# Reordering one pair's work in the pipelined recurrence: what TensorE, ScalarE, VectorE and GpSimd do two pairs ahead

## The reference

```python
xa = layernorm(x); sx = previous_row(xa) - xa
xxx = tanh((xa + sx * maa_x) @ maa_w1)             # low rank, 5 x 32
xm = xa + sx * (maa_stack + xxx @ maa_w2)           # five mixtures: k, w, v, r, g
w = exp(-exp(time_decay + tanh(xw @ td_w1) @ td_w2))
r, k, v, g = xr @ Wr.T, xk @ Wk.T, xv @ Wv.T, silu(xg @ Wg.T)
s = s * w_t + k_t v_t ; out_t = r_t . (u * k_t v_t + s_before)   # scan over 128 tokens, 32 heads of 8 x 8
x1 = x + (groupnorm(out) * g) @ Wo.T
xc = layernorm(x1); sx2 = previous_row(xc) - xc
rr = sigmoid((xc + sx2 * maa_r) @ Wfr.T); kk = relu((xc + sx2 * maa_k) @ Wfk.T) ** 2
return x1 + rr * (kk @ Wfv.T)                       # the feed-forward part
```

## Time and profile before

| | us |
|---|---|
| median of 3 runs (2198.15 to 2201.47) | 2199.23 |
| the profiled execution's own time | 2204.45 |
| its span, first to last instruction | 2202.7 |
| mean granted TensorE clock over the span | 0.955 of full |
| recurrence stage within the span | about 1837 to 2202.7 |

### The profile page before, as it was taken

The page is one execution under the profiler, slowest core; times in us unless marked ns, Lnnn a source line. Parts: engine busy times, 40 slices in busy tenths (PEclk is TensorE's granted clock), DMA queues, the critical chain, the costliest instruction groups (busy, mean ns, idle before and its releaser), DMA issues. The chain is left out here.

```text
span 2202.7 us, 41115 instructions
## 1 busy us (share of the span) xinstructions
PE 1982.4 (90%) x15672; PEld 1724.6 (78%) x15672; DVE 1282.7 (58%) x2577; ACT 1085.0 (49%) x2926; POOL 529.4 (24%) x359
## 2 busy tenths in 40 slices
PE   5997898798999999999899999999979896888975
PEld 4675676796999999999699999999969884565653
DVE  5886787235555555555565554555533374888883
ACT  3775687563534433443454333433356432466653
POOL 3543554454200000000240000000025323324230
PEclk9998999899999999999999999999989997899986
DMA  4001000400000000002200000000120000000000
GB/s 164 2 2 30 21 11 2 153 1 6 6 6 5 0 5 5 5 5 87 72 6 6 0 5 5 5 5 0 46 69 1 11 29 0 1 6 10 6 10 10
DMA packets 33884, 44.90 MB, mean 20 GB/s; under 512 B 2178, under 2 KB 25828, under 8 KB 33508
## 3 DMA queue, kind: packets, MB, share of 16 engines
q1 hardware_dynamic: 33764, 43.26, 5.8%
HBM read 32.76 MB, written 2.10 MB: 16 GB/s over the span
## 5 line engine op out<-in xcount | busy, mean ns | idle before, releaser
L815 DVE TENSOR_TENSOR w_head_lo<-banks,w_head_hi 128x512 fp32r<-128x512 f32 x128 | 88.2, 691 | 249.3 <-ACT w_head_hi L727 241.7
L781 DVE TENSOR_TENSOR arena<-banks,cols 128x512 f32<-128x512 f32 x128 | 88.5, 692 | 227.3 <-PE banks L118 227.2
L746 ACT ACTIVATE arena<-banks 128x512 f32<-128x512 f32 x128 | 74.7, 595 | 296.4 <-PE banks L605 292.1
L524 POOL TENSOR_TENSOR w_hT_lo<-arena,w_hT_hi 128x512 fp32r<-128x512 f32 x16 | 20.9, 1304 | 821.6 <-ACT w_hT_hi L701 821.6
L739 ACT ACTIVATE arena<-banks,arena 128x129 f32<-128x129 f32 x512 | 180.6, 374 | 39.8 <-DVE arena L795 39.8
L989 POOL TENSOR_TENSOR arena<-arena 128x1024 f32<-128x1024 f32 x64 | 150.3, 2375 | 139.1 <-DVE arena L1248 139.1
L727 ACT ACTIVATE w_head_hi<-banks 128x512 fp32r<-128x512 f32 x128 | 76.4, 597 | 196.6 <-PE banks L615 196.5
L1182 ACT ACTIVATE arena<-arena 128x128 f32<-128x128 f32 x512 | 162.5, 394 | 3.5 <-DVE arena L1257 3.4
L116 PE MATMUL banks<-w_wo_lo,w_head_hi 128*128 128x256 f32 x512 | 148.6, 290 | 1.3 <-DVE w_head_lo L815 1.3
L116 PE MATMUL banks<-w_hT_lo,w_hi 128*128 128x256 f32 x512 | 146.6, 286 | 0.0
L116 PE MATMUL banks<-w_kv_lo,w_hi 128*128 128x256 f32 x512 | 145.2, 284 | 0.2
(11 more groups left out here) (300 smaller groups left out, 5831.0 us busy)
## 6 DMA issues: line engine op xcount, KB each, us to landing
arena<-ctx_t SPq DMA_DIRECT2D x32, 256.0 KB, 2.5
arena<-in_L_xattn_wq SPq DMA_DIRECT2D x8, 512.0 KB, 4.8
arena<-in_L_xattn_wk SPq DMA_DIRECT2D x8, 512.0 KB, 5.9
arena<-in_L_xattn_wv SPq DMA_DIRECT2D x8, 512.0 KB, 7.4
arena<-in_L_xattn_wo SPq DMA_DIRECT2D x8, 512.0 KB, 9.7
x<-in_x SPq DMA_DIRECT2D x4, 512.0 KB, 5.4
arena<-in_L_xattn_w SPq DMA_DIRECT2D x2, 1024.0 KB, 11.2
ctx_t<-in_ctx_t SPq DMA_DIRECT2D x1, 2048.0 KB, 12.5
```

Source lines behind the costliest of these rows:

```text
L746: act.activation(probT[:, b, :, :], bank[5 + b][:, :].rearrange("p (h q) -> p h q", h=HG), ACT.Copy).then_inc(probT_ok, 1)
L781: dve.tensor_tensor(qT[:, h:h + 2, :], bank[use % 2][:, :].rearrange("p (h t) -> p h t", h=2), core.col(bias, g * HG + h, 2)[:, :, None].t ...
L815: dve.tensor_tensor(head_lo[:, two, :], bank[5 + half][:, :].rearrange("p (h t) -> p h t", h=2), head_hi[:, two, :], ALU.subtract).then_in ...
```

## The change

Only the order of the steps within a slot changes, with one wait more on GpSimd; no instruction of arithmetic is added or taken away.

- TensorE: a_transpose(p + 2) moves from behind project_rr to ahead of project_kk; a_low(p + 2) moves from between centre and variance to right behind project_ff, ahead of unit 3's sum_heads, spread_v(p + 1, 0) and bonus_sums.
- ScalarE: tanh_low comes ahead of square_centred; normalise(p + 2) moves up ahead of row_rstd; copy_xa(p + 2) moves ahead of square_relu and sigmoid_rr.
- VectorE: shift_a(p + 2) moves ahead of unit 3.
- GpSimd: multiply_rk(a) also waits until kv_ok has reached 4a, which is when weigh_keys of unit 3 of the pair before has ended.

```diff
--- before.py
+++ after.py
@@ -1878,6 +1878,7 @@
                 gp.wait_ge(read["r"], a + 1)
                 gp.wait_ge(read["k"], a + 1)
                 wait(gp, ready["c"], a)
+                wait(gp, kv_ok, a * UNITS)
                 gp.tensor_tensor(rk[:, :, :], rT[:, parity(a), :, :], kT[:, parity(a), :, :], ALU.mult).then_inc(rk_ok, 1)
 
             def add_xa(a, fs):
@@ -2110,13 +2111,14 @@
                     c_transpose(p - 1)
                 if u:
                     sum_heads(p, 2)
+                if exists(p + 2):
+                    a_transpose(p + 2)
                 if c:
                     project_kk(p - 1)
                     project_rr(p - 1)
+                    project_ff(p - 1)
                 if exists(p + 2):
-                    a_transpose(p + 2)
-                if c:
-                    project_ff(p - 1)
+                    a_low(p + 2)
                 if u:
                     sum_heads(p, 3)
                 if a:
@@ -2126,9 +2128,6 @@
                     bonus_sums(p + 1)
                 if u:
                     centre(p)
-                if exists(p + 2):
-                    a_low(p + 2)
-                if u:
                     variance(p)
 
             core.wait_loaded(pe, stage, "maa_w1", "maa_w2", "maa_w2g")
@@ -2259,11 +2258,10 @@
 
             def slot(p):
                 u, a, c = exists(p), exists(p + 1), exists(p - 1)
-                if c:
-                    square_centred(p - 1)
                 if a:
                     tanh_low(p + 1)
                 if c:
+                    square_centred(p - 1)
                     group_rstd(p - 1)
                 if u:
                     make_decay(p, 2)
@@ -2276,6 +2274,8 @@
                     copy_v(p + 1)
                 if u:
                     make_decay(p, 3)
+                if exists(p + 2):
+                    normalise(p + 2)
                 if c:
                     row_rstd(p - 1)
                 if a:
@@ -2290,12 +2290,10 @@
                 if a:
                     make_decay(p + 1, 0)
                 if exists(p + 2):
-                    normalise(p + 2)
+                    copy_xa(p + 2)
                 if c:
                     square_relu(p - 1)
                     sigmoid_rr(p - 1)
-                if exists(p + 2):
-                    copy_xa(p + 2)
                 if u:
                     copy_raw(p)
                 if a:
@@ -2442,10 +2440,10 @@
                     make_gate(p + 1)
                 if c:
                     shift_c(p - 1)
+                if exists(p + 2):
+                    shift_a(p + 2)
                 if u:
                     unit(p, 3)
-                if exists(p + 2):
-                    shift_a(p + 2)
                 if c:
                     gate_ff(p - 1)
```

## The result

| | before | changed |
|---|---|---|
| median of 7 runs, us | 2200.72 | 2206.28 |
| lowest to highest, us | 2198.15 to 2201.47 | 2204.08 to 2210.02 |
| the profiled execution's own time, us | 2204.45 | 2204.08 |
| its span, us | 2202.7 | 2202.4 |

The ratio is 1.0028, with a 95% interval of 1.0016 to 1.0040: 6 us slower, 3.5 to 8.8. The forecast was 2203.5 in a range of 2194 to 2210.

A forecast was written before the change was run, and what follows sets the result against it. Neither TensorE nor VectorE alone was taken as the bound, but a loop passing between them. Slots -2.8, start +3.9 and clock +3.2 gave +4.3 on 2199.2, so 2203.5 us, range 2194 to 2210.

The forecast's parts named there:

- The new loop, 37.04 us at full clock: Slots 1 to 5: the loop from one VectorE mix to the next takes 37.04 us, against 37.6 before.
- Slot -1, +2.5 with 4.4 as the upper bound: Slot -1: spread_v behind a_low starts VectorE's unit 0 1.4 us later, plus 1.1 for clock; +4.4 if all at half clock.
- the 1.1 us for the clock: Slot -1: 1.1 us added for half clock after TensorE's idling, since a 2.07 us gap was followed by half clock.
- Slot 0, +1.4: Slot 0: unit 3's heads come 3.9 us later; the mix is +2.65 at the same clock, +0.1 at full; +1.4 taken.
- The slots, -2.8: Slots 1 to 5: a loop of 37.04 us against 37.6, five times, saves 2.8 us.
- two such drops more than before: Slots 1 to 5: two more clock drops around the mixing products, at 1.6 us each: +3.2, bounds 0 and +8.
- rival 4: It does nothing: project_kk stays at half clock, unit 3's heads 0.8 us later, slots 37.8, total 2201.7 us; chance 0.10.
- Transposes ahead of project_kk don't bring it forward: TensorE's 2.07 us wait splits into some 0.4 and 1.1; project_kk still starts at 2009.72, when shift_c ends.
- The hold moves the stall and nobody gains: GpSimd's r k moves beside unit 3's scan: unit 3's VectorE product takes 2.11 us; unit 2's lost 1.09 gained nothing.
- rival 2: Unit 3's product isn't stalled, 1.23 us: 0.7 less in five slots, 0.9 in slot 0; 2193.5 us; chance 0.18.
- normalise "costs nothing": ScalarE: normalise fits ahead of row_rstd's wait at no cost, as ScalarE is busy 24 of 37.6 us.
- the signs that the prediction named: Right: project_kk about 2 us, two gaps, unit 3's product near 2.1, 0.69 wait, slot 1's mix two to five us later.

The follow-up runs named there:

- experiment 5: Changed kernel with one unused 128x256 product in each of TensorE's two short waits ahead of project_kk, from slot 1 on; ratio 1.0025 to the kernel before.
- Experiment 4: Changed kernel with eight unused products filling TensorE's gap in slot -1, between the transposes and a_low; ratio 1.0019 to the kernel before.
- experiment 7: Kernel before with three unused products in the 2.07 us wait ahead of project_kk, nothing else changed; ratio 0.9978.
- experiments 2 and 8: First: changed kernel without GpSimd's added wait (the hold), 1.0031. Second: kernel before with that wait alone added, 1.0002. Both ratios are to the kernel before.
- experiment 6: Changed order from slot 1 on only, no hold, three unused 128-row products in the mix: 1.0006; with unused products at project_kk too: 0.9997.
- the early normalise: Kernel before with normalise(p + 2) alone moved ahead of row_rstd on ScalarE; ratio 0.9968 to the kernel before.

## Why the prediction was right, point by point

- *The new loop, 37.04 us at full clock.* Right: 36.99 in slot 3 and 36.98 in three slots of experiment 5. Its steps: unit 3's product 2.11 (2.11 forecast), heads waiting 0.63 (0.7), variance 0.69 (0.69), shift_a without a wait.
- *Slot -1, +2.5 with 4.4 as the upper bound.* Measured +4.5, and this was the largest error. The step that was mis-sized is the 1.1 us for the clock: I took what a gap of 2.07 us had cost, and after 4.0 us of idling the whole low-rank product and nearly the whole of spread_v ran at half clock. Experiment 4 gives 2.7 for the clock and 1.8 for the order (1.4 forecast).
- *Slot 0, +1.4.* Measured +1.7. With slot -1 that is +6.2 for the start, for +3.9 in bounds of +1.5 and +7.1.
- *The slots, -2.8.* The length of the loop was right, but the -2.8 sets it at full clock against an average over slots that partly ran at half clock. At the same clock the change makes a slot 0.85 longer (36.98 for 36.14, slot 4 of before), and that is the hold's price (experiment 7). The prediction took "a gap of 2.07 was followed by half clock" from slot 3; in slot 4 the same gap was followed by full clock.
- *The clock in the slots, "two such drops more than before", +3.2.* Wrong in kind. Both kernels have one drop around the mix; what stayed besides is project_kk at half clock in three slots of five, at 0.85 each, the price that rival 4 gave for it (0.8). A drop around the mix costs 1.3, not 1.6 (38.30 for 36.99; the average of 37.28 had slot 4 in it). And two drops "more than before" would be three, since -2.8 had taken out the one of before as well. Measured against 36.98 the clock costs 3.9 in the five slots, so that -2.8 + 3.2 = +0.4 came near the measured +0.8. That is luck: the term was for drops that didn't come, and left out those that did.
- *Transposes ahead of project_kk don't bring it forward.* Right: it still starts when shift_c is done (21.66 us after the mix in slot 3; 21.83 before).
- *The hold moves the stall and nobody gains.* Right: unit 2's product went from 2.32 to 1.23 us and unit 3's from 1.23 to 2.11 (experiments 2 and 8). At full clock the hold even costs, 0.85 in the new order and 0.6 in the old; the prediction had 0.7 for it, as rival 2's gain. The rule that the prediction cited from the Trainium skill, "SBUF — State Buffer", section "SBUF: two separate sides", agrees: once GpSimd's product starts beside unit 3's scan, it is unit 3's product that takes 2.11 us.
- *Rival 2* didn't come true in the changed kernel, where unit 3's product took 2.11. Its price was right when the hold was taken out (36.32 at full clock), but its gain failed to come: from slot 2 on the slots are 1.2 us longer, with the k and v projections at half clock.
- *normalise "costs nothing".* True, and short of the truth: alone it is worth 3 us in the first two slots.

Of the signs that the prediction named, unit 3's product at 2.11, unit 2's at 1.23, the two gaps and the wait of 0.69 were all seen. project_kk at about 2 us was seen in two slots of five; in the other three it stayed near 3.45, which was to be a sign of being wrong. From the first mix, that of slot 1 comes 6.2 us later, over the two to five named.

The sum, +4.3, lies under the measured 6 us (3.5 to 8.8) mainly by the 2.0 us of slot -1. The forecast of 2203.5 was counted from a median before of 2199.23 (3 runs); seven runs gave 2200.72. Not settled: why a drop lands at project_kk in one slot and at the projections in another; no run separates position in time from what went before.

## What to carry to other kernels

Walk through the first and last turns of a software pipeline by themselves: an order that is hidden where all parts are present can put a wait in front of everything where one is missing, and here those two turns decided. Moving work ahead of a wait helps only if the thing waited for comes earlier; look at what the next engine is then late with. When a step brings an engine back to full clock, compare slots at equal clock before crediting the order: here the change made them 0.85 us longer, and three unused products in the wait, with the old order, made the kernel 5 us faster.

## What the runs showed of the hardware that was not expected

TensorE's half clock came back in another place when the wait ahead of project_kk was filled. In experiment 7 the drop appeared at low_rate and the k and v projections in each slot from 2 on, 5.8 us for 3.7, and in slots 2 to 5 TensorE was never idle for more than 0.60 us at a time. Nor does a wait always bring the drop: with the same 2.07 us ahead of it, project_kk ran at full clock in slot 4 of before and in slots 1, 3 and 6 of the early normalise. In experiment 7 what ran just ahead of the drop were the ten mixing products of 32 rows:

```profile
1981.70 1.14 PE L2005 MATMUL banks<-arena 32*128 32x256 f32 x8
1983.44 2.31 PE L2005 MATMUL banks<-arena 32*128 32x256 f32 x12 [0.60 <-ACT arena L2224]
1986.19 1.97 PE L2012 MATMUL banks<-arena 128*64 128x256 f32 x4 [0.45 <-POOL arena L1887]
1988.09 5.81 PE L1970 MATMUL banks<-arena 128*128 128x256 f32 x16
```

With products of 128 rows among them (experiment 6) the projections ran at 3.72 us in four slots of five. Whether those products kept the clock up, or only moved the slots in time, isn't shown.
